# Attention radial weights from a plain input, y0 multiplied in PSUM by ScalarE, and two y copies moved in VectorE's order

## The chip, the cores and the metric

The program runs on one core of one Trainium2 chip. The metric is device time in microseconds from the first to the last instruction of that core; less is better.

## What is computed

The reference is two layers of an equivariant graph network. The first is attention over 206,250 edges; the change lies there. For each edge a radial vector of 16 numbers (`rbf`) is multiplied by `W_rbf` to give 224 weights, and these scale the edge's message by way of `y0` and `y1`, the edge's spherical harmonics:

```
w1 = rbf @ W_rbf                       # ss 64 | sv 64 | vs 32 | vv0 32 | vv1 32
out_s = concat[w_ss * s * y0,  w_vv0 * (v . y1) / sqrt3]
out_v = concat[(w_sv * s) y1,  w_vs * v * y0,  w_vv1 * cross(v, y1) / sqrt2]
```

So `y0` belongs to two of the five parts, `ss` and `vs`, which are 96 of the 224 columns. The rest of the layer (logits, softmax, values, a second product with `y`, the sum over edges) and the second layer stay as they are.

## The kernel before

`attention_edges` works through 404 tiles of 512 edges (`SUPER = 404`), each as 4 blocks of 128 edges with the edges in partitions. Every engine has one loop, unrolled four times, and its order is written out by hand. A step `t = m + d` in the body of iteration `m` says that this engine does that piece of work for tile `m + d`; so one iteration mixes pieces of some six tiles. Engines are tied by counting semaphores alone. "An iteration" below is one pass of an engine through this body.

The names that matter, with the lines of the kernel before:

- **SyncE** loads `rin` (L452), the gather indices, `y_early` (L460) and `y_late` (L466), and stores `hout` (L471). **GpSimd** gathers 4 + 4 blocks of node rows for each tile (L484, L487), and may start on a tile once VectorE has summed the tile four before it (semaphore `summed`, L586).
- **Radial weights.** `rin` holds, for each tile, 64 rows of 512 columns: on the left `rbf` twice, on the right y0 and ones. VectorE multiplies left by right into `rbfy` (L537). TensorE multiplies `rbfy` by `wy` into `b_w`, banks 0 and 1 of PSUM (L697); it first waits for VectorE's last reader of `b_w`, L556 (`first_done`). VectorE reads `b_w` one iteration later (L547 to L556) to make `first`.
- **TensorE's order from the weights on:** weights (L697), transposes of the second block of `second` (`turn2(t,1)`, L639), `maps(t,1)` (L647 to L649), third transposes (`turn2(t,2)`, L639 on `nodes`), then in the next body the first transposes of `first` (L630), `values_of(t,0)` (L657 to L659), more transposes, `values_of(t,1)`, `maps(t,0)`, `turn2(t,0)` (L639 on `ae_second`), and the weights again. `values_of(t,0)` waits until ScalarE has copied the third transposes out (`kept2`).
- **ScalarE's order over the same stretch:** `keep2(t,1)` (L729, copies the second transposes out of PSUM), four activations that scale `gated` by y0 (L781), `keep2(t,2)` (L729), `keep_maps(t,1)` (L718 to L720), `keep1(t,0)` (L725).
- **The small copies on VectorE:** `ya` (L534), `yb` (L575) and `yc` (L580) bring y values into bank 7 of PSUM, where the products with y (L514, L566, L602) read them.

The buffer `spare`, which the profile names `nodes`, holds `gated`.

Of the kernel before, what the change touches and what calls it, by code (L numbers as in the profile page):

```python
# [21 lines left out]
ALU = mybir.AluOpType  # L22
# [5 lines left out]
P = 128  # L28
# [352 lines left out]
def attention_edges(nc, g):  # L381

    w, psum, banks, io = g["w"], g["psum"], g["banks"], g["io"]
    with ExitStack() as ctx:
        def sb(name, shape, dt=F32):
            return ctx.enter_context(nc.sbuf_tensor(f"ae_{name}", shape, dt))

        def sem(name):
# [7 lines left out]
        rin = [sb(f"rin{u}", [64, 512]) for u in range(4)]  # L396
        rbfy = [sb(f"rbfy{u}", [64, 256]) for u in range(2)]
# [20 lines left out]
        ya_done, yb_done, yc_done, summed, spread, outer_done, cross_done, dot_done, first_done = (sem(x) for x in (  # L418
            "ya_done", "yb_done", "yc_done", "summed", "spread", "outer_done", "cross_done", "dot_done", "first_done"))
# [6 lines left out]
        kept, mapped_kept, scaled, kept2, values_kept, yy_kept, logit_kept = (sem(x) for x in (  # L426
            "kept", "mapped_kept", "scaled", "kept2", "values_kept", "yy_kept", "logit_kept"))
# [17 lines left out]
        with nc.Block() as block:  # L445
            @block.sync
            def _(sp):
                def body(m):
                    t = m + 4
                    if t.inside(SUPER):  # L450
                        wait(sp, spread, t.n - 3)
                        sp.dma_start(rin[t.slot4][:, :], io["rin"][t.n]).then_inc(rin_in[t.slot4], 16)  # L452
# [40 lines left out]
            def _(dve):  # L493
# [10 lines left out]
                def body(m):  # L504
# [26 lines left out]
                    if t.inside(SUPER):  # L531
                        dve.wait_ge(early_in[t.slot4], 16 * (t.quarter + 1))
                        wait(dve, outer_done, t.n)
                        dve.tensor_copy(ya, y_early[t.slot4][:, :, 1:6]).then_inc(ya_done, 1)  # L534
                        dve.wait_ge(rin_in[t.slot4], 16 * (t.quarter + 1))
                        wait(dve, pe_weights, t.n - 1)
                        dve.tensor_tensor(rbfy[t.slot][:, :], rin[t.slot4][:, 0:256], rin[t.slot4][:, 256:512], ALU.mult)\  # L537
                            .then_inc(spread, 1)
                    t = m
                    if t.inside(SUPER):  # L540
# [4 lines left out]
                        dve.wait_ge(pe_weights, t.n + 1)  # L545
                        wait(dve, pe_turned, 3 * t.n - 3)
                        dve.tensor_tensor(out[:, :, 0:384 - P].rearrange("p k (a c) -> p k a c", c=CS)[:, :, 0:4:3, :],  # L547
                                          b_w[:, :, 0:P].rearrange("p k (a c) -> p k a c", a=2),
                                          msg[:, :, 0:CS].unsqueeze(2).to_broadcast([P, 4, 2, CS]), ALU.mult)
                        dve.tensor_tensor(comps(out[:, :, 256:352]), b_w[:, :, 192:224].unsqueeze(2).to_broadcast(three),  # L550
                                          comps(msg[:, :, CS:C]), ALU.mult)
                        dve.wait_ge(cross_done, t.n + 1)
                        dve.tensor_tensor(comps(out[:, :, 96:192]), b_w[:, :, 160:192].unsqueeze(2).to_broadcast(three),
                                          cross[:, :, :, :], ALU.mult)
                        dve.wait_ge(dot_done, t.n + 1)
                        dve.tensor_tensor(out[:, :, CS:96], b_w[:, :, P:160], dot[:, :, :], ALU.mult).then_inc(first_done, 1)  # L556
# [31 lines left out]
                    if t.inside(SUPER):  # L588
# [7 lines left out]
                        dve.tensor_reduce(dot[:, :, :], diag[:, :, :, :].rearrange("p k x c -> p k c x"), AX, ALU.add).then_inc(rest_done, 1)  # L596
                    t = m + -4
# [28 lines left out]
            def _(pe):  # L626
# [35 lines left out]
                def body(m):  # L662
# [50 lines left out]
            def _(act):  # L713
# [24 lines left out]
                def body(m):  # L738
# [34 lines left out]
                    if t.inside(SUPER):  # L773
                        keep2(t, 1)
                    t = m + -2
# [14 lines left out]
                loop(act, body, 0, SUPER + 4, SUPER, 4)  # L790
# [498 lines left out]
def lay_pack(i):  # L1289
# [13 lines left out]
    for lo in (0, 32):  # L1303
        W["wy"][lo:lo + 16, 0:64], W["wy"][lo:lo + 16, 192:224] = ss, vs
        W["wy"][lo + 16:lo + 32, 64:128], W["wy"][lo + 16:lo + 32, 128:160], W["wy"][lo + 16:lo + 32, 160:192] = sv, vv0, vv1
# [40 lines left out]
def lay_inputs(i):  # L1346
# [16 lines left out]
    rbf = np.pad(np.asarray(i["edge_attr_16"]), ((0, E - EDGES), (0, 0))).reshape(SUPER, 2, 256, 16).transpose(0, 1, 3, 2)  # L1363
    y0 = np.broadcast_to(y[:, :, 0].reshape(SUPER, 2, 1, 256), rbf.shape)
    left = np.concatenate([rbf, rbf], 2).reshape(SUPER, 64, 256)
    right = np.concatenate([y0, np.ones_like(rbf)], 2).reshape(SUPER, 64, 256)
# [4 lines left out]
        rin=np.concatenate([left, right], 2), yall=y.reshape(4 * SUPER, P, 4).transpose(1, 0, 2),  # L1371
# [21 lines left out]
```

## Time and profile before

| | |
|---|---|
| median of 3 runs | 8659.92 us (8658.96 to 8663.35) |
| the profiled execution, own time | 8654.65 us |
| its span | 8652.9 us |
| granted clock of TensorE, mean | 0.943 |
| busy: TensorE / VectorE / ScalarE / GpSimd | 83% / 88% / 60% / 64% |
| the attention edge loop | about 264 to 4637 us of the span |

The span holds stages with different limits, so shares over the whole say little about the attention loop; the rows further down take that loop alone. Durations of neighbouring instructions on one engine overlap a little: where the time that an instruction costs its engine is wanted, read the distance from its start to the next start.

### The profile page before, as it was taken

The page shows a single profiled execution, that of the slowest core. Times are in us where ns is not written, and L with a number is a line of the kernel's source. Part 1 is how long each engine was busy: PE and PEld are TensorE (multiplying, and loading weights), DVE is VectorE, ACT ScalarE, POOL GpSimd, SP SyncE. Part 2 cuts the span into 40 slices and gives each one's busy share as a digit, 9 for nine tenths or more (in the row PEclk, how much of TensorE's full clock was granted, in tenths as well). Part 3 has the DMA queues.
Part 4 walks back from the last instruction along what each step waited for, and adds up shares of the span by engine and source line. Part 5 has one row for each costly group of instructions (what it writes and reads, how often), then busy time and mean ns, then how long its engine had stood idle before and what let it go on. Part 6 is the DMA issues. An engine that isn't in the chain of part 4 may idle for free. (4 is left out here: it accounts for less than half of the span.)

```text
span 8652.9 us, 204396 instructions
## 1 busy us (share of the span) xinstructions
PE 7203.1 (83%) x48374; PEld 5958.3 (69%) x48374; DVE 7624.6 (88%) x18883; ACT 5158.5 (60%) x17363; POOL 5527.0 (64%) x5949
## 2 busy tenths in 40 slices
PE   4799999999999999999996677756888888888885
PEld 2688888888888888888885566633555555555555
DVE  3799999999999999999998555534999999999993
ACT  1466666666666666666664211112777777777771
POOL 0677777777777777777772677702777777777750
PEclk5799999999999999999998999955999999999995
DMA  1343333333333333333331566601333333333330
GB/s 71 92 109 106 105 105 106 105 105 106 106 105 106 105 105 106 105 105 105 106 105 57 170 181 181 181 3 47 92 88 89 89 89 89 88 89 89 88 72 19
DMA packets 854921, 859.39 MB, mean 99 GB/s; under 512 B 480448, under 2 KB 637760, under 8 KB 854208
## 3 DMA queue, kind: packets, MB, share of 16 engines
q0 software_dynamic: 241920, 413.20, 19.6%
q1 hardware_dynamic: 612928, 445.36, 18.0%
q8 instruction: 28, 0.46, 0.0%
q14 instruction: 45, 0.37, 0.0%
HBM read 709.51 MB, written 148.44 MB: 99 GB/s over the span
## 5 line engine op out<-in xcount | busy, mean ns | idle before, releaser
L1157 POOL DMA_INDIRECT ce_node<-tab_conv,ce_idx x1808 | 1708.7, 945 | 1059.8 <-issue 654.3
L484 POOL DMA_INDIRECT ae_gsrc<-tab_src,ae_idx x1616 | 1537.2, 951 | 890.6 <-issue 449.7
L487 POOL DMA_INDIRECT ae_gdst<-tab_dst,ae_idx x1616 | 1635.6, 1012 | 541.3 <-issue 539.4
L1247 PE MATMUL psum<-ce_prod,ce_plain 128*128 128x384 f32 x3616 | 1540.5, 508 | 337.8 <-DVE ce_prod L1220 275.1
L1232 ACT ACTIVATE ce_prod<-ce_raw,ce_y 128x64 f32<-128x64 f32 x5424 | 1465.1, 333 | 0.0
L1230 ACT ACTIVATE ce_prod<-ce_raw,ce_y 128x160 f32<-128x160 f32 x1808 | 753.4, 417 | 527.9 <-DVE ce_raw L1179 527.9
L729 ACT ACTIVATE ae_second_t<-psum 128x512 f32<-128x512 f32 x1212 | 731.5, 604 | 502.2 <-PE psum L639 496.2
L1249 PEld LDWEIGHTS psum<-ce_prod,ce_plain 128*128 128x128 f32 x3616 | 688.0, 190 | 479.9 <-issue 2.1
L1247 PEld LDWEIGHTS psum<-ce_prod,ce_plain 128*128 128x128 f32 x3616 | 547.2, 191 | 484.8 <-DVE ce_plain L1208 346.1
L647 PE MATMUL psum<-pack_sb,ae_first_t 128*128 128x200 f32 x3232 | 851.8, 345 | 2.2 <-ACT ae_first_t L725 2.0
L1008 PE MATMUL psum<-ag_exval,ag_hot 128*128 128x164 f32 x3616 | 615.3, 314 | 223.9 <-issue 116.2
L657 PE MATMUL psum<-pack_sb,ae_second_t 128*128 128x96 f32 x3232 | 664.4, 287 | 129.0 <-ACT ae_second_t L729 125.0
L1008 PEld LDWEIGHTS psum<-ag_exval,ag_hot 128*128 128x128 f32 x3616 | 514.6, 190 | 324.6 <-DVE agg L997 131.3
L725 ACT ACTIVATE ae_first_t<-psum 128x512 f32<-128x512 f32 (+1 forms) x1212 | 690.2, 607 | 40.8 <-PE psum L630 40.5
L697 PE MATMUL psum<-pack_sb,ae_rbfy 32*128 32x224 f32 x3232 | 418.2, 372 | 297.7 <-DVE ae_first L556 276.2
L630 PE MATMUL psum<-pack_sb,ae_first 128*128 128x128 f32 (+1 forms) x4848 | 664.7, 274 | 0.0
L657 PEld LDWEIGHTS psum<-pack_sb,ae_second_t 128*128 128x128 f32 x3232 | 486.0, 190 | 240.9 <-issue 164.6
L1249 PE MATMUL psum<-ce_prod,ce_plain 128*128 128x96 f32 x3616 | 647.0, 261 | 0.0
L649 PE MATMUL psum<-pack_sb,ae_first_t 96*128 96x96 f32 x3232 | 626.8, 276 | 0.0
L659 PE MATMUL psum<-pack_sb,ae_second_t 128*128 128x96 f32 x3232 | 625.4, 275 | 0.0
L658 PE MATMUL psum<-pack_sb,ae_second_t 128*128 128x96 f32 x3232 | 625.3, 275 | 0.0
L735 ACT ACTIVATE ae_values<-psum 128x256 f32<-128x256 f32 x808 | 310.5, 384 | 522.1 <-PE psum L659 522.1
(179 smaller groups left out, 19883.6 us busy)
## 6 DMA issues: line engine op xcount, KB each, us to landing
ag_val<-h_dram SPq DMA_DIRECT2D x452, 320.0 KB, 3.2
h_dram<-ae_hout SPq DMA_DIRECT2D x404, 320.0 KB, 2.2
ce_query<-in_query SPq DMA_DIRECT2D x452, 128.0 KB
ae_rin<-in_rin SPq DMA_DIRECT2D x404, 128.0 KB
ce_node<-tab_conv,ce_idx POOLq DMA_INDIRECT x1808
ae_gsrc<-tab_src,ae_idx POOLq DMA_INDIRECT x1616
ae_gdst<-tab_dst,ae_idx POOLq DMA_INDIRECT x1616
nodes<-in_x SPq DMA_DIRECT2D x2, 3920.0 KB, 14.0
```

What stands on the lines that cost most here:

```text
L484: pool.indirect_dma_start(gsrc[t.slot4][:, k, :], None, g["tab_src"], bass.IndirectOffsetOnAxis(ap=idx[t.slot4][:, k:k + 1], axis=0))\
L487: pool.indirect_dma_start(gdst[t.slot4][:, k, :], None, g["tab_dst"], bass.IndirectOffsetOnAxis(ap=idx[t.slot4][:, 4 + k:5 + k], axis=0))\
L647: pe.matmul(b_m[:, i, 0:200], first_t[0][:, e], w("m1_0"), start=True, stop=False)
L657: pe.matmul(b_h[:, i, 0:96], second_t[0][:, e], w("m2_0"), start=True, stop=False, skip_group_check=True)
L725: act.activation(first_t[b][0:rows, :], b_t[b % 2][0:rows, :], ACT.Copy).then_inc(kept, 1)
L729: act.activation(second_t[b][:, :], b_t[(b + 1) % 2][:, :], ACT.Copy).then_inc(kept2, 1)
L1008: ins = pe.matmul(banks[t.slot4][:, 0:W], hot[t.slot4][:, k, :], exval[t.slot4][:, k, :], start=(k == 0), stop=(k == 3))
L1157: pool.indirect_dma_start(node[t.slot8][:, k, :], None, g["tab_conv"], bass.IndirectOffsetOnAxis(ap=idx[t.slot8][:, k:k + 1], axis=0))\
L1230: act.activation(prod[t.slot][:, k, 0:160], raw[t.slot][:, k, 0:160], ACT.Identity, scale=y[t.slot8][:, k, 0:1])
L1232: ins = act.activation(prod[t.slot][:, k, 192 + 96 * x:256 + 96 * x], raw[t.slot][:, k, 160:WW], ACT.Identity, scale=y[t.slot8][:, k, x + ...
L1247: pe.matmul(b_a[t.slot], plain[t.slot4][:, k, :], prod[t.slot][:, k, 96:480], start=(k == 0), stop=False, skip_group_check=True)
L1249: ins = pe.matmul(b_a[t.slot][:, 96:384].rearrange("p (x c) -> p x c", x=3)[:, :, CS:96], plain[t.slot4][:, k, :], prod[t.slot][:, k, 0:96 ...
```

## The change

`rin` becomes 64 rows of 256 columns: `rbf` and 16 rows of zeros for each half, with no y0 in it. VectorE's multiplication (L537) and its buffer go, and TensorE takes `rin` straight from the load. The columns of the weights are put in another order, `vs, ss, sv, vv0, vv1`, so that the 96 that need y0 stand first. ScalarE then multiplies these 96 columns by y0, in place in PSUM, with four activations for a tile, and signals `weighted`, for which VectorE waits in the place of `pe_weights`. On VectorE the copy `yb` moves from between L569 and L586 to behind the reduction L596; the copy `yc` moves from behind `yb` to behind `ya`, where L537 stood. ScalarE's loop starts one body earlier.

```diff
-        rin = [sb(f"rin{u}", [64, 512]) for u in range(4)]
-        rbfy = [sb(f"rbfy{u}", [64, 256]) for u in range(2)]
+        rin = [sb(f"rin{u}", [64, 256]) for u in range(4)]
...
@@ SyncE
-                        wait(sp, spread, t.n - 3)
+                        wait(sp, pe_weights, t.n - 3)
                         sp.dma_start(rin[t.slot4][:, :], io["rin"][t.n]).then_inc(rin_in[t.slot4], 16)
@@ VectorE
                         dve.tensor_copy(ya, y_early[t.slot4][:, :, 1:6]).then_inc(ya_done, 1)
-                        dve.wait_ge(rin_in[t.slot4], 16 * (t.quarter + 1))
-                        wait(dve, pe_weights, t.n - 1)
-                        dve.tensor_tensor(rbfy[t.slot][:, :], rin[t.slot4][:, 0:256], rin[t.slot4][:, 256:512], ALU.mult)\
-                            .then_inc(spread, 1)
+                    t = m + -4
+                    if t.inside(SUPER):
+                        dve.wait_ge(late_in[t.slot4], 16 * (t.quarter + 1))
+                        wait(dve, path2_done, t.n)
+                        dve.tensor_copy(yc, y_late[t.slot4][:, :, 2:5]).then_inc(yc_done, 1)
...
-                        dve.wait_ge(pe_weights, t.n + 1)
+                        dve.wait_ge(weighted, t.n + 1)
...
-                    t = m + -1
-                    if t.inside(SUPER):
-                        dve.wait_ge(early_in[t.slot4], 16 * (t.quarter + 1))
-                        wait(dve, outer2_done, t.n)
-                        dve.tensor_copy(yb, y_early[t.slot4][:, :, 1:6]).then_inc(yb_done, 1)
-                    t = m + -4
-                    if t.inside(SUPER):
-                        dve.wait_ge(late_in[t.slot4], 16 * (t.quarter + 1))
-                        wait(dve, path2_done, t.n)
-                        dve.tensor_copy(yc, y_late[t.slot4][:, :, 2:5]).then_inc(yc_done, 1)
...
                         dve.tensor_reduce(dot[:, :, :], diag[:, :, :, :].rearrange("p k x c -> p k c x"), AX, ALU.add).then_inc(rest_done, 1)
+                    t = m + -1
+                    if t.inside(SUPER):
+                        dve.wait_ge(early_in[t.slot4], 16 * (t.quarter + 1))
+                        wait(dve, outer2_done, t.n)
+                        dve.tensor_copy(yb, y_early[t.slot4][:, :, 1:6]).then_inc(yb_done, 1)
@@ TensorE
-                        pe.wait_ge(spread, t.n + 1)
+                        pe.wait_ge(rin_in[t.slot4], 16 * (t.quarter + 1))
...
-                            ins = pe.matmul(b_w[:, k, :], rbfy[t.slot][q:q + 32, e:e + P], w("wy")[q:q + 32, :], start=True, stop=True)
+                            ins = pe.matmul(b_w[:, k, :], rin[t.slot4][q:q + 32, e:e + P], w("wy")[q:q + 32, :], start=True, stop=True)
@@ ScalarE, between keep2(m - 3, 1) and the scaling of gated for m - 2
+                    t = m + 1
+                    if t.inside(SUPER):
+                        act.wait_ge(pe_weights, t.n + 1)
+                        act.wait_ge(early_in[t.slot4], 16 * (t.quarter + 1))
+                        for k in range(4):
+                            ins = act.activation(b_w[:, k, 0:96], b_w[:, k, 0:96], ACT.Identity, scale=y_early[t.slot4][:, k, 0:1])
+                        ins.then_inc(weighted, 1)
...
-                loop(act, body, 0, SUPER + 4, SUPER, 4)
+                loop(act, body, -1, SUPER + 4, SUPER, 4)
```

ScalarE's order of before, in the looped body, from the copies of logit and yy to the copies of the maps; `ae_second_t` is the copied transposes, `nodes` read by L781 is `gated`:

```order
L766 ACTIVATE alpha<-ae_logit 128x16 [waits ae_logit_done]
L771 ACTIVATE ae_yy<-yy 128x4 [waits ae_outer2_done]
L729 ACTIVATE ae_second_t<-psum 128x512 [waits ae_pe_turned2]
L781 ACTIVATE ae_second<-nodes,ae_y_late 128x192 [waits ae_pe_turned2,ae_late_in2,ae_gate_done]
L781 ACTIVATE ae_second<-nodes,ae_y_late 128x192 x3
L729 ACTIVATE ae_second_t<-psum 128x512 [waits ae_pe_turned2]
L718 ACTIVATE ae_mapped<-psum 128x2x72 [waits ae_pe_mapped]
```

The same place in ScalarE's order of the change (line numbers shift by five, L724 is `keep2`, L783 the scaling of `gated`):

```order
L761 ACTIVATE alpha<-ae_logit 128x16 [waits ae_logit_done]
L766 ACTIVATE ae_yy<-yy 128x4 [waits ae_outer2_done]
L724 ACTIVATE ae_second_t<-psum 128x512 [waits ae_pe_turned2]
L775 ACTIVATE psum<-psum,ae_y_early 128x96 [waits ae_early_in1,ae_pe_weights]
L775 ACTIVATE psum<-psum,ae_y_early 128x96 x3
L783 ACTIVATE ae_second<-nodes,ae_y_late 128x192 [waits ae_pe_turned2,ae_late_in2,ae_gate_done]
L783 ACTIVATE ae_second<-nodes,ae_y_late 128x192 x3
L724 ACTIVATE ae_second_t<-psum 128x512 [waits ae_pe_turned2]
L713 ACTIVATE ae_mapped<-psum 128x2x72 [waits ae_pe_mapped]
```

Four activations now stand between the copy of the second transposes and the scaling of `gated`, ahead of the copy of the third transposes.

VectorE's order of before, from the end of the second set of products with y to the third:

```order
L569 TENSOR_TENSOR ae_bent<-nodes,ae_yy 128x128 [waits ae_bent_done,ae_yy_kept]
L575 COPY psum<-ae_y_early 128x20 [waits ae_outer2_done,ae_early_in0]
L580 COPY psum<-ae_y_late 128x12 [waits ae_path2_done,ae_late_in1]
L586 TENSOR_TENSOR ae_msg<-ae_gsrc,ae_gdst 128x640 [waits ae_outer_done,ae_first_done,ae_gathered2]
L593 TENSOR_TENSOR nodes<-ae_plus,psum 128x4x2x32 [waits ae_first_done,ae_pe_turned2,ae_outer2_done]
L595 TENSOR_TENSOR ae_second<-ae_plus,psum 128x4x32
L596 TENSOR_REDUCE ae_dot<-ae_diag 128x128
L602 TENSOR_TENSOR ae_path<-ae_values,psum 128x384 [waits ae_values_done,ae_yc_done,ae_values_kept]
```

The same place in VectorE's order of the change:

```order
L569 TENSOR_TENSOR ae_bent<-nodes,ae_yy 128x128 [waits ae_bent_done,ae_yy_kept]
L576 TENSOR_TENSOR ae_msg<-ae_gsrc,ae_gdst 128x640 [waits ae_outer_done,ae_first_done,ae_gathered2]
L583 TENSOR_TENSOR nodes<-ae_plus,psum 128x4x2x32 [waits ae_first_done,ae_pe_turned2,ae_outer2_done]
L585 TENSOR_TENSOR ae_second<-ae_plus,psum 128x4x32
L586 TENSOR_REDUCE ae_dot<-ae_diag 128x128
L591 COPY psum<-ae_y_early 128x20 [waits ae_outer2_done,ae_early_in0]
L597 TENSOR_TENSOR ae_path<-ae_values,psum 128x384 [waits ae_values_done,ae_yc_done,ae_values_kept]
```

Both copies have gone from between the product L569 and the sum of the gathered rows; one of them now stands ahead of the third product.

## Rows read from the trace of the kernel before

**Rows 1.** Windows: PE, PEld, DVE, ACT, POOL busy; clock, DMA share, GB/s.

```profile
320.00:4410.00 4090.00, 3723.18 (x30180) 3433.20 (x30177) 4043.47 (x10561) 2747.59 (x8300) 2977.02 (x3033) 1.00 0.40 106
```

**Rows 2.** One line's instructions over the whole span: the sum L586, once a tile.

```profile
L586 DVE TENSOR_TENSOR ae_msg<-ae_gsrc,ae_gdst x404: 809/826/827, 263.9 to 4637.1; 128x640 f32<-128x640 f32 x135
```

**Rows 3.** Waits from 1000 to 4000 us: total, times, longest.

```profile
ACT ae_second_t L729 <- PE psum L639: 345.1, 277, 1.4
...
PE psum L697 <- DVE ae_first L556: 183.9, 277, 0.8
...
PE psum L657 <- ACT ae_second_t L729: 85.9, 277, 0.3
```

**Rows 4.** Timeline of one iteration, TensorE (PE, PEld) and ScalarE.

```profile
2010.72 0.68 PEld L697 LDWEIGHTS psum<-pack_sb,ae_rbfy 32*128 32x128 f32 x8 [0.84 <-DVE ae_first L556]
...
2012.37 0.60 ACT L729 ACTIVATE ae_second_t<-psum 128x512 f32<-128x512 f32 x1 [1.18 <-PE psum L639]
...
2012.87 1.48 ACT L781 ACTIVATE ae_second<-nodes,ae_y_late 128x192 f32<-128x192 f32 x4
...
2013.61 0.47 PEld L639 LDWEIGHTS psum<-pack_sb,nodes 128*128 128x128 f32 x4
2013.72 0.60 PE L639 MATMUL psum<-pack_sb,nodes 128*128 128x128 f32 x4
...
2014.06 0.47 PEld L630 LDWEIGHTS psum<-pack_sb,ae_first 128*128 128x128 f32 x4
...
2014.36 0.60 ACT L729 ACTIVATE ae_second_t<-psum 128x512 f32<-128x512 f32 x1
...
2015.09 0.30 PEld L657 LDWEIGHTS psum<-pack_sb,ae_second_t 128*128 128x128 f32 x2 [0.56 <-issue]
...
2020.19 0.47 PEld L639 LDWEIGHTS psum<-pack_sb,ae_second 128*128 128x128 f32 x4
```

**Rows 5.** Timeline of VectorE around L537 and around the two copies.

```profile
2007.96 0.17 DVE L534 COPY psum<-ae_y_early 128x20 f32<-128x20 f32 x1
2008.04 0.40 DVE L537 TENSOR_TENSOR ae_rbfy<-ae_rin 64x256 f32<-64x256 f32 x1
2008.37 0.57 DVE L543 TENSOR_REDUCE ae_dot<-ae_diag 128x128 f32<-128x384 f32 x1
...
2011.99 0.27 DVE L569 TENSOR_TENSOR ae_bent<-nodes,ae_yy 128x128 f32<-128x128 f32 x1
2012.36 0.18 DVE L575 COPY psum<-ae_y_early 128x20 f32<-128x20 f32 x1
2012.49 0.17 DVE L580 COPY psum<-ae_y_late 128x12 f32<-128x12 f32 x1
2012.70 0.83 DVE L586 TENSOR_TENSOR ae_msg<-ae_gsrc,ae_gdst 128x640 f32<-128x640 f32 x1
```

**Rows 6.** Timeline of GpSimd: the first and the last gather of one tile.

```profile
2003.44 0.94 POOL L484 DMA_INDIRECT ae_gsrc<-tab_src,ae_idx  x1 [0.84 <-DVE ae_msg L586]
...
2012.55 0.95 POOL L487 DMA_INDIRECT ae_gdst<-tab_dst,ae_idx  x1 [0.30 <-issue]
```

**Rows 7.** Timeline of ScalarE elsewhere: L299, L301 and L1232 scale by a column.

```profile
84.72 0.35 ACT L301 ACTIVATE tab_feat<-psum,pack_sb 96x128 f32<-96x128 f32 x1
84.97 0.45 ACT L299 ACTIVATE tab_feat<-psum,pack_sb 64x128 f32<-64x128 f32 x1
...
6012.57 0.81 ACT L1232 ACTIVATE ce_prod<-ce_raw,ce_y 128x64 f32<-128x64 f32 x3
```

**Rows 8.** Timeline of ScalarE: a plain copy out of PSUM, and its successor.

```profile
2014.86 0.28 ACT L718 ACTIVATE ae_mapped<-psum 128x144 f32<-128x144 f32 x1
2015.03 0.34 ACT L719 ACTIVATE nodes<-psum 128x192 f32<-128x192 f32 x1
```

**Rows 9.** Groups by line on ScalarE, whole span: count, busy us, mean ns, idle.

```profile
L1232 ACT ACTIVATE ce_prod<-ce_raw,ce_y 128x64 f32<-128x64 f32 x5424 | 1465.1, 333 | 0.0
...
L781 ACT ACTIVATE ae_second<-nodes,ae_y_late 128x192 f32<-128x192 f32 x1616 | 598.0, 444 | 0.0
```

More of the change, by code:

```diff
@@ L416, in attention_edges @@
         filled, may_gather = sem("filled"), sem("may_gather")
-        ya_done, yb_done, yc_done, summed, spread, outer_done, cross_done, dot_done, first_done = (sem(x) for x in (
-            "ya_done", "yb_done", "yc_done", "summed", "spread", "outer_done", "cross_done", "dot_done", "first_done"))
+        ya_done, yb_done, yc_done, summed, outer_done, cross_done, dot_done, first_done = (sem(x) for x in (
+            "ya_done", "yb_done", "yc_done", "summed", "outer_done", "cross_done", "dot_done", "first_done"))
         gate_done, outer2_done, bent_done, rest_done, scored_done, logit_done, path2_done, values_done = (sem(x) for x in (
@@ L424, in attention_edges @@
             "pe_weights", "pe_turned", "pe_mapped", "pe_turned2", "pe_values"))
-        kept, mapped_kept, scaled, kept2, values_kept, yy_kept, logit_kept = (sem(x) for x in (
-            "kept", "mapped_kept", "scaled", "kept2", "values_kept", "yy_kept", "logit_kept"))
+        weighted, kept, mapped_kept, scaled, kept2, values_kept, yy_kept, logit_kept = (sem(x) for x in (
+            "weighted", "kept", "mapped_kept", "scaled", "kept2", "values_kept", "yy_kept", "logit_kept"))
         b_w = psum[:, 0:2, :].rearrange("p b (k c) -> p (b k) c", c=256)[:, :, 0:WY]
@@ L544, in body @@
                             .then_inc(dot_done, 1)
-                        dve.wait_ge(pe_weights, t.n + 1)
+                        dve.wait_ge(weighted, t.n + 1)
                         wait(dve, pe_turned, 3 * t.n - 3)
                         dve.tensor_tensor(out[:, :, 0:384 - P].rearrange("p k (a c) -> p k a c", c=CS)[:, :, 0:4:3, :],
-                                          b_w[:, :, 0:P].rearrange("p k (a c) -> p k a c", a=2),
+                                          b_w[:, :, 32:160].rearrange("p k (a c) -> p k a c", a=2),
                                           msg[:, :, 0:CS].unsqueeze(2).to_broadcast([P, 4, 2, CS]), ALU.mult)
-                        dve.tensor_tensor(comps(out[:, :, 256:352]), b_w[:, :, 192:224].unsqueeze(2).to_broadcast(three),
+                        dve.tensor_tensor(comps(out[:, :, 256:352]), b_w[:, :, 0:32].unsqueeze(2).to_broadcast(three),
                                           comps(msg[:, :, CS:C]), ALU.mult)
                         dve.wait_ge(cross_done, t.n + 1)
-                        dve.tensor_tensor(comps(out[:, :, 96:192]), b_w[:, :, 160:192].unsqueeze(2).to_broadcast(three),
+                        dve.tensor_tensor(comps(out[:, :, 96:192]), b_w[:, :, 192:224].unsqueeze(2).to_broadcast(three),
                                           cross[:, :, :, :], ALU.mult)
                         dve.wait_ge(dot_done, t.n + 1)
-                        dve.tensor_tensor(out[:, :, CS:96], b_w[:, :, P:160], dot[:, :, :], ALU.mult).then_inc(first_done, 1)
+                        dve.tensor_tensor(out[:, :, CS:96], b_w[:, :, 160:192], dot[:, :, :], ALU.mult).then_inc(first_done, 1)
                     t = m + -2
@@ L1361, in lay_inputs @@
     ey6 = y.reshape(SUPER, 4, P, 4)[..., [0, 1, 2, 3, 1, 2]].transpose(0, 2, 1, 3).reshape(SUPER, P, 24)
[L1363 to L1366, printed above, removed]
+    rbf = np.pad(np.asarray(i["edge_attr_16"]), ((0, E - EDGES), (0, 16))).reshape(SUPER, 2, 256, 32).transpose(0, 1, 3, 2)
     query = np.pad(np.asarray(i["edge_attr_64"]), ((0, E - EDGES), (0, 0))).reshape(SUPER, 2, 256, 64)
@@ L1370, in lay_inputs @@
         pack=lay_pack(i), x=x, eidx=eidx, ey6=ey6, sdst=sdst, dst3=dst3,
-        rin=np.concatenate([left, right], 2), yall=y.reshape(4 * SUPER, P, 4).transpose(1, 0, 2),
+        rin=rbf.reshape(SUPER, 64, 256), yall=y.reshape(4 * SUPER, P, 4).transpose(1, 0, 2),
         query=query)
```

3 lines of the change are left out of this document (1 added, 2 removed).

## The prediction

> **What bounds the kernel now.** I read the page first, for where the engines are busy: VectorE has the most, TensorE is close behind (the table above). Over the whole span that mixes stages, so next I took the attention loop alone. There VectorE is busy 4043 of 4090 us (98.9%), TensorE 3723 (91.0%), GpSimd 2977 (72.8%), ScalarE 2748 (67.2%), with TensorE's granted clock at 1.00 throughout [rows 1]. The length of an iteration comes from one line that runs once a tile: 404 sums, first at 263.9 and last at 4637.1 us, so (4637.1 - 263.9) / 403 = 10.85 us [rows 2]. Then the list of waits: VectorE has none in it. TensorE waits for VectorE's L556 in every iteration, 183.9 / 277 = 0.66 us, and for ScalarE's copy of the transposes, 85.9 / 277 = 0.31 us; ScalarE waits 1.25 us for TensorE [rows 3]; GpSimd waits for VectorE's sum [rows 6]. Three engines wait for VectorE or for each other and VectorE for none: VectorE sets the pace, with TensorE only some tenths behind it. So whatever VectorE sheds is gained only until the next loop of dependences is as long. There are three to measure.
>
> **VectorE's own length afterwards.** L537 costs it the distance to the next start, 2008.37 - 2008.04 = 0.33 us. From L569 to L586 it takes 12.70 - 11.99 = 0.71 us, though the product, 0.27 us long, is followed only by two copies on 20 and 12 columns: L575 starts 0.10 us after L569 has ended, because it waits for that end [rows 5]. With both copies gone the sum waits only for older things; I put it 0.25 us behind L569, which gives 0.46. The copies come back elsewhere at 0.08 (L534 to L537) to 0.21 us each (L580 to L586) [rows 5]; I take 0.25 for both. The net is -0.33 - 0.46 + 0.25 = -0.54, that is 10.31 us; with the ends 10.2 to 10.45.
>
> **GpSimd's own length.** Its eight gathers start 9.11 us apart from first to last (2003.44 to 2012.55), seven steps, or 1.30 each; the eighth step brings 10.4 us. It now waits 0.84 us at the head of each tile instead of the usual 0.30, for the sum that VectorE moves earlier [rows 6]. It would be at most 10.4 us, and it is three tiles ahead.
>
> **The ring of TensorE and ScalarE.** This is the one the change lengthens. Weights (L697) load at 2010.72. Behind them on TensorE stand the second transposes; ScalarE starts to copy these at 2012.37, so 1.65 us after. Its next start is 0.50 later (2012.87). Four scalings of `gated` take 1.48 with the last at full length, 0.444 [rows 9], so one step is (1.48 - 0.444) / 3 = 0.345. Then comes the copy of the third transposes, 0.60 long, and 0.13 us after its end (2014.96) TensorE loads for `values_of` at 2015.09. From there it runs without a wait to 2020.19, and four more transposes at the pace of 2013.61 to 2014.06 bring it to the next weights: 5.10 + 0.45 = 5.55 us [rows 4]. The third copy starts at 2014.36 today because the third transposes end only at 13.72 + 0.60 = 14.32 [rows 4]; with ScalarE later that end is no longer what it waits for, and the four scalings count 4 x 0.345 = 1.38. All together 1.65 + 0.50 + 1.38 + 0.60 + 0.13 + 5.55 = 9.81 us, plus w for the four new activations, which are queued just ahead of the scalings. Today this ring has about 1 us to spare against 10.85; everything hangs on w.
>
> **The price of w.** The trace has no scaling within PSUM. Nearest is L301, which reads PSUM, scales by a column of SBUF and has 128 columns: its successor starts 84.97 - 84.72 = 0.25 us later [rows 7]. Fewer columns are cheaper: L1232 at 64 columns steps by (0.81 - 0.333) / 2 = 0.24, L781 at 192 by 0.345, so (0.345 - 0.24) / 128 = 0.00082 us a column [rows 4, 7, 9]. For 96 columns that is 0.25 - 32 x 0.00082 = 0.22, and w = 4 x 0.22 = 0.89. From below, a plain copy out of PSUM steps by 15.03 - 14.86 = 0.17 at 144 columns [rows 8], 0.13 at 96, so w = 0.52. From above, priced as a scaling that reads SBUF, 0.24 + 32 x 0.00082 = 0.27 and w = 1.07. The value taken is that of L301: same source, same kind of scale, only the destination differs. The wait for `pe_weights` ahead of them costs nothing, since TensorE has done the second transposes, which stand behind the weights, before ScalarE even begins its copy; `y_early` was loaded two iterations before. Behind the four are queued the scalings of `gated`, the third copy and both `keep` copies; TensorE's `values_of` waits for the third copy.
>
> The Trainium skill, "ScalarE: Activation LUTs", section "What ACT_TABLE_LOAD costs", gives an activation 186 ns + 0.833 ns a column, 93 ns more for a scale column, and 93 ns of overlap with the next. By that 96 columns cost 0.27 us each, an estimate of w = 1.06. L301's 0.35 us is under the 0.386 that this rule gives for 128 columns. The sum by the rule is the second rival's.
>
> **The rest at nothing.** `rin` has half the bytes and is waited for by TensorE instead of VectorE; it is loaded four tiles ahead. SyncE's waits move: `rin` now follows `pe_weights`, about 3 us later in its round than L537 was, `y_early` follows the later `yb`; each is needed two or more iterations on, so 10 us or more of cover against a few. Should the cover of `rin` go, TensorE would stand at the weights for the lateness of the load. VectorE's new wait for `weighted`: the four are done about 1.65 + 0.50 + 0.89 = 3.0 us after the weights began, and VectorE's readers of `b_w` come behind L543, which starts at 2008.37 [rows 5], or 2019.2 one iteration later, 8.5 us after that mark. TensorE's weights take the same time, since neither rows nor columns of the matmul change.
>
> **The sum.** The ring is 9.81 + 0.89 = 10.70 us, longer than VectorE's 10.31 and GpSimd's 10.4, so it becomes the pace. 10.85 - 10.70 = 0.15 us, times 404 is 61 us. Against the profiled execution's own 8654.65 that is 8594; the median of the runs shown is 5 us above it, so **8599 us**, 0.7% less. VectorE sheds 218 us, and some 157 of them turn into its new waits. The measurement of this kernel can tell about 0.2%, 17 us, from no change, so the sign turns at 10.81 for faster and at 10.89 for slower, that is w = 1.00 and 1.08.
>
> **Rivals.**
>
> 1. *The ring does not close.* If the activations cost as little as a plain copy, w = 0.52, the ring is 10.33 us and GpSimd's 10.4 sets the pace: 0.45 x 404 = 182 us, 8478. Against it speaks L301, which steps by 0.25 us at 128 columns where the plain copy steps by 0.17 at 144 [rows 7, 8]: scaling by a column is not free. Chance 0.09.
> 2. *The activations cost as those that read SBUF.* Then w = 1.07, the ring 10.88, +0.03 x 404 = +12 us: 8672, within 0.2%, and the kernel has only changed its bound. This is what the page of the Trainium skill named above comes to. Chance 0.15.
> 3. *Slower: the four in-place activations don't overlap.* All four read and write the same two banks; if each had to end before the next reads, each costs its duration, about 0.35 - 0.03 = 0.32 us by L301 [rows 7], w = 1.29, the ring 11.10, +0.25 x 404 = +101 us: 8761. Slower is decided from w = 1.08 on, 0.27 an activation. For it: nothing in the trace reads and writes PSUM on ScalarE. Against: plain copies that follow one another through one pair of banks overlap freely [rows 8]. Chance 0.11.
>
> **Chances and range.** The forecast has 0.65: w from 0.80 to 1.00, so 10.61 to 10.81 us, 8563 to 8644. Faster by over 0.2% takes the forecast and rival 1, less what of the forecast lies at its upper edge: 0.72. Within 0.2% 0.16, slower 0.12. The range goes from part of the way to rival 1 up over rival 2, 8520 to 8682, and leaves out rival 3 and most of rival 1.
>
> **What would show it.** Distance of L576, the sum, from tile to tile: 10.70. The new line L775: 1616 instructions, mean about 320 ns, step 0.22. In the list of waits TensorE's wait for VectorE's L556 is gone; its wait for ScalarE's L724 grows from 0.31 to some 0.8 us an iteration, since TensorE's own work is 10.85 - 0.66 - 0.31 = 9.88. VectorE's busy share in the loop falls from 98.9% to about 96%, with a wait for ScalarE's maps or for `weighted`. ScalarE's third copy starts right behind L783, with no wait for TensorE. L569 to the sum: 0.25 instead of 0.71. If VectorE is still without waits and the iteration is under 10.5, the ring was mis-sized; if the step of L775 is over 0.27, rival 3 holds. The forecast is wrong too if TensorE's stretch from `values_of` to the weights, 5.55 here, meets new waits of its own once VectorE is earlier.

## The result and the profile after

The changed kernel takes 8676.86 us (median of 16 runs, 8674.66 to 8681.44), the kernel before in the same measurement 8660.35 us (16 runs). The ratio is 1.002, with a 95% interval of 1.0012 to 1.0027. The forecast was 8599 us, 0.7% less; what came is 0.2% more. It is inside the range of 8520 to 8682, but the interval puts it on the other side of no change.

The iteration first. The sum of the gathered rows, now L576, once a tile, over the whole span of the changed kernel:

```profile
L576 DVE TENSOR_TENSOR ae_msg<-ae_gsrc,ae_gdst x404: 807/817/827, 262.7 to 4655.8; 128x640 f32<-128x640 f32 x135
```

(4655.8 - 262.7) / 403 = 10.90 us, where it was 10.85 [rows 2]. From first to last sum the loop is 19.9 us longer; the medians differ by 16.5 us and the two profiled spans by 26.3. The windows of the same stretch as [rows 1], with the same columns:

```profile
320.00:4410.00 4090.00, 3676.82 (x30011) 3406.49 (x30010) 3870.52 (x10132) 3030.45 (x9758) 3024.84 (x3019) 1.00 0.37 99
```

VectorE has fallen from 98.9% to 94.6% (about 96% was forecast) and ScalarE has risen from 67.2% to 74.1%; TensorE's granted clock is 1.00 in both. So VectorE did shed its work, and it was no longer busy all the time. Who waits for whom, from 1000 to 4000 us of the changed kernel (total, times, longest):

```profile
PE psum L652 <- ACT ae_second_t L724: 302.6, 275, 1.1
...
DVE nodes L520 <- ACT ae_mapped L715: 161.5, 275, 0.8
ACT ae_second_t L724 <- PE psum L634: 141.8, 275, 0.5
```

TensorE's wait for VectorE's L556 [rows 3] is gone from the list. Its wait for ScalarE's third copy has grown from 0.31 to 302.6 / 275 = 1.10 us an iteration (some 0.8 was forecast), and VectorE, which waited for nobody, now waits 0.59 us for ScalarE's copies of the maps. These rows fit the forecast's picture, that the pace has passed from VectorE to the ring of TensorE and ScalarE; the experiments below test it. The ring is longer than forecast. It can be read off one iteration of the changed kernel, start by start (columns: start, length, engine, line):

```profile
2006.12 0.47 PEld L634 LDWEIGHTS psum<-pack_sb,ae_second 128*128 128x128 f32 x4
2006.76 0.68 PEld L692 LDWEIGHTS psum<-pack_sb,ae_rin 32*128 32x128 f32 x8 [0.17 <-issue]
...
2007.71 0.42 PEld L634 LDWEIGHTS psum<-pack_sb,ae_second 128*128 128x128 f32 x4 [0.28 <-issue]
...
2008.41 0.60 ACT L724 ACTIVATE ae_second_t<-psum 128x512 f32<-128x512 f32 x1 [0.52 <-PE psum L634]
2008.90 1.00 ACT L775 ACTIVATE psum<-psum,ae_y_early 128x96 f32<-128x96 f32 x4
2009.80 1.51 ACT L783 ACTIVATE ae_second<-nodes,ae_y_late 128x192 f32<-128x192 f32 x4
2011.18 0.61 ACT L724 ACTIVATE ae_second_t<-psum 128x512 f32<-128x512 f32 x1
...
2011.91 0.30 PEld L652 LDWEIGHTS psum<-pack_sb,ae_second_t 128*128 128x128 f32 x2 [1.35 <-issue]
...
2017.02 0.48 PEld L634 LDWEIGHTS psum<-pack_sb,ae_second 128*128 128x128 f32 x4
2017.66 0.68 PEld L692 LDWEIGHTS psum<-pack_sb,ae_rin 32*128 32x128 f32 x8 [0.16 <-issue]
```

| step of the ring | forecast | measured |
|---|---|---|
| weights to ScalarE's second copy | 1.65 | 1.65 |
| that copy | 0.50 | 0.49 |
| four activations in PSUM (w) | 0.89 | 0.90 |
| four scalings of `gated` | 1.38 | 1.38 |
| third copy, and TensorE's load after it | 0.73 | 0.73 |
| TensorE from `values_of` to `turn2(t,0)` | 5.10 | 5.11 |
| from `turn2(t,0)` to the weights | 0.45 | 0.64 |
| sum | 10.70 | 10.90 |

Six of seven steps came within 0.01 us. The seventh is 0.19 us too short. The row to look at is L692: it begins 0.64 us after the four transposes' first load, and 0.16 us after the end of their last, with no engine named as releaser. In the kernel before, TensorE stood there anyway, 0.84 us for VectorE [rows 4], and the 0.19 us lay under that wait.

VectorE came out close to the forecast. From L569 to the sum it now takes 0.20 us (0.25 was forecast), and the copies, L591 and L538, cost 0.08 us each in their new places (0.25 for both was forecast):

```profile
2006.50 0.28 DVE L569 TENSOR_TENSOR ae_bent<-nodes,ae_yy 128x128 f32<-128x128 f32 x1
2006.70 0.82 DVE L576 TENSOR_TENSOR ae_msg<-ae_gsrc,ae_gdst 128x640 f32<-128x640 f32 x1
...
2008.47 0.17 DVE L591 COPY psum<-ae_y_early 128x20 f32<-128x20 f32 x1
2008.55 0.54 DVE L597 TENSOR_TENSOR ae_path<-ae_values,psum 128x384 f32<-128x384 f32 x1
...
2010.87 0.55 DVE L513 TENSOR_TENSOR ae_plus<-ae_msg,psum 128x384 f32<-128x384 f32 x1
2011.33 0.56 DVE L513 TENSOR_TENSOR psum<-ae_msg,psum 128x384 f32<-128x384 f32 x1
2012.65 0.69 DVE L520 TENSOR_TENSOR nodes<-ae_mapped,nodes 128x512 f32<-128x512 f32 x1 [0.76 <-ACT ae_mapped L715]
...
2013.87 0.16 DVE L538 COPY psum<-ae_y_late 128x12 f32<-128x12 f32 x1
2013.95 0.58 DVE L543 TENSOR_REDUCE ae_dot<-ae_diag 128x128 f32<-128x384 f32 x1
```

L520 starts 1.32 us after the last L513 instead of the 0.46 at which these follow one another; in this iteration VectorE loses 0.86 us there. The mean step over the loop, taken from all such starts, is 1.14 us, so 0.68 us lost, and VectorE's own work is 10.90 - 0.68 = 10.22 us an iteration (10.31 forecast).

### The profile page after: what moved, and what is told of

The parts are those of the page before. It is cut to its first block and busy times, and to the rows that moved or that the text cites. A ratio compares the mean times of both kernels' runs of the same rounds, so it can differ in the third digit from the quotient of the medians.

```text
span 8679.2 us, 205804 instructions
## 1 busy us (share of the span) xinstructions
PE 7175.0 (83%) x48374; PEld 5950.2 (69%) x48374; DVE 7461.0 (86%) x18479; ACT 5479.1 (63%) x18979; POOL 5591.7 (64%) x5949
## 5 line engine op out<-in xcount | busy, mean ns | idle before, releaser
L486 POOL DMA_INDIRECT ae_gdst<-tab_dst,ae_idx x1616 | 1701.8, 1053 | 530.5 <-issue 530.5
L1249 PE MATMUL psum<-ce_prod,ce_plain 128*128 128x384 f32 x3616 | 1539.8, 508 | 338.1 <-DVE ce_prod L1222 275.4
L1232 ACT ACTIVATE ce_prod<-ce_raw,ce_y 128x160 f32<-128x160 f32 x1808 | 753.2, 417 | 526.9 <-DVE ce_raw L1181 526.9
L1249 PEld LDWEIGHTS psum<-ce_prod,ce_plain 128*128 128x128 f32 x3616 | 547.0, 191 | 485.1 <-DVE ce_plain L1210 343.1
L724 ACT ACTIVATE ae_second_t<-psum 128x512 f32<-128x512 f32 x1212 | 737.9, 609 | 208.5 <-PE psum L634 208.4
L720 ACT ACTIVATE ae_first_t<-psum 128x512 f32<-128x512 f32 (+1 forms) x1212 | 699.8, 617 | 1.1 <-PE psum L625 1.1
L783 ACT ACTIVATE ae_second<-nodes,ae_y_late 128x192 f32<-128x192 f32 x1616 | 608.2, 474 | 0.0
```

The lines of the kernel that those rows point to most:

```text
L486: pool.indirect_dma_start(gdst[t.slot4][:, k, :], None, g["tab_dst"], bass.IndirectOffsetOnAxis(ap=idx[t.slot4][:, 4 + k:5 + k], axis=0))\
L720: act.activation(first_t[b][0:rows, :], b_t[b % 2][0:rows, :], ACT.Copy).then_inc(kept, 1)
L724: act.activation(second_t[b][:, :], b_t[(b + 1) % 2][:, :], ACT.Copy).then_inc(kept2, 1)
L1232: act.activation(prod[t.slot][:, k, 0:160], raw[t.slot][:, k, 0:160], ACT.Identity, scale=y[t.slot8][:, k, 0:1])
L1249: pe.matmul(b_a[t.slot], plain[t.slot4][:, k, :], prod[t.slot][:, k, 96:480], start=(k == 0), stop=False, skip_group_check=True)
```

## The experiments

Two theories stand at the start. **The ring**: the loop of TensorE and ScalarE in the table above is the pace, each activation stands in it with its full step, and 0.19 us of it is the way into the radial weights. **VectorE by way of the maps**: the pace is VectorE's chain, which now waits at L520 for ScalarE's copies of the maps, and these stand behind the four activations. Both fit a time of 8677 us.

Of 18 runs, three give times that can be set beside the change's: e5, e6 and e16. The other 15 ran on chips where the kernel before itself took 12,200 to 13,000 us instead of 8660. There an iteration takes 17.8 to 19.9 us on average, in every kernel, and ScalarE idles for microseconds ahead of copies for which the trace names no engine of the core as releaser. Two of its rows in e17:

```profile
3884.53 0.60 ACT L725 ACTIVATE ae_first_t<-psum 128x512 f32<-128x512 f32 x1 [2.27 <-remote]
3887.39 0.59 ACT L725 ACTIVATE ae_first_t<-psum 96x512 f32<-96x512 f32 x1 [2.26 <-remote]
```

TensorE idles too, and its granted clock goes to and fro between 1.00 and 0.50, its levels of 2.4 and 1.2 GHz. Windows of e17, with the columns of [rows 1]:

```profile
320.00:4410.00 4090.00, 2884.18 (x18057) 2615.88 (x18057) 2409.85 (x6342) 1675.93 (x4971) 1795.27 (x1812) 0.76 0.23 63
...
3876.00:3882.00 6.00, 0.00 (x0) 0.00 (x0) 2.21 (x7) 0.29 (x2) 4.48 (x6) 0.50 0.28 64
```

Over the attention loop the clock is 0.76 of full speed where it was 1.00, and in the 6 us ahead of the rows above TensorE runs no matmul and stands at 0.50. These delays drown the ring, so a ratio of two such times says nothing about this question. From those runs I use distances between neighbouring instructions, at a granted clock of 1.00, and whole iterations without a stall. Two of these stand at the end of every run: the last two distances from sum to sum, at a granted clock of 1.00 and, in these 15, with all gathers done. Where the whole loop is undisturbed they agree with its mean: 10.91 us in the changed kernel, 10.35 in e5 and 10.45 in e16. Only in the kernel before do they not, with 11.16 and 10.80.

**The activations behind the third copy** (e3, and e5 where it counts). The block is taken out from ahead of the scalings and put behind `keep2(t, 2)`:

```diff
 keep2(m - 3, 1)
-four activations on b_w (t = m + 1), weighted + 1
 scaling of gated (t = m - 2)
 keep2(m - 3, 2)
+four activations on b_w (t = m + 1), weighted + 1
 keep_maps(m - 1, 1)
```

> The changed kernel with the four in-place activations moved behind the copy of the third transposes (and ahead of the copies of the maps), so that TensorE no longer waits for them. Theory of the ring: it shrinks by 0.89 to 10.0 us, plus about 0.2 because the copy of the first transposes is now late for TensorE; then VectorE's 10.3 or GpSimd's 10.4 us is the pace: about 8677 - 0.5 x 404 = 8475 us. Rival (the pace is the wait of VectorE for ScalarE's copies of the maps, which stand behind the activations in either order): unchanged, 10.90 us and 8677 us.

> The kernel of e3 once more, since on the chip of the first four runs the kernel before itself took 12828 us. The changed kernel with the four in-place activations behind the copy of the third transposes. Theory of the ring: about 10.4 us an iteration, 8475 us. Rival (the pace is VectorE's wait for ScalarE's copies of the maps, which stand behind the activations in either order): unchanged, 10.90 us and 8677 us.

e3 is one of the 15 (12545 us); its last two iterations take 10.35 us. e5 took 8458.34 us against 8655.42 before on the same chip, ratio 0.9773 (0.9757 to 0.979). The sum's line and two waits of e5:

```profile
L576 DVE TENSOR_TENSOR ae_msg<-ae_gsrc,ae_gdst x404: 807/820/843, 263.2 to 4436.0; 128x640 f32<-128x640 f32 x135
```

```profile
PE psum L652 <- ACT ae_second_t L724: 89.9, 290, 0.3
...
PEld psum L625 <- ACT ae_first_t L720: 74.7, 290, 0.3
...
DVE nodes L520 <- ACT ae_mapped L715: 15.0, 73, 0.2
```

10.35 us an iteration. The activations still stand ahead of the maps here, so the second theory falls: it had forecast no change. TensorE's wait for the third copy is back to 0.31 us, and the wait on L720 (74.7 / 290 = 0.26 us) is the lateness of the first transposes' copy that the expectation names. So the ring can be read off this kernel too:

```profile
2003.90 0.68 PEld L692 LDWEIGHTS psum<-pack_sb,ae_rin 32*128 32x128 f32 x8 [0.17 <-issue]
...
2006.90 0.60 PE L634 MATMUL psum<-pack_sb,nodes 128*128 128x128 f32 x4
...
2007.54 0.60 ACT L724 ACTIVATE ae_second_t<-psum 128x512 f32<-128x512 f32 x1
...
2008.26 0.30 PEld L652 LDWEIGHTS psum<-pack_sb,ae_second_t 128*128 128x128 f32 x2 [0.56 <-issue]
...
2014.25 0.68 PEld L692 LDWEIGHTS psum<-pack_sb,ae_rin 32*128 32x128 f32 x8 [0.16 <-issue]
```

From the weights to the third copy it takes 3.64 us, 0.12 more than 1.65 + 0.49 + 1.38 = 3.52, because the third transposes end only at 2007.50, as in the kernel before; 0.72 to TensorE's load; and 5.99 to the next weights, 0.24 more than 5.11 + 0.64 = 5.75, because of L720. Together that is 10.35. The four activations have not left the ring altogether: of their 0.90 us they still cost 0.24, by way of L720. GpSimd waits for VectorE no more, and its gathers fill the iteration; but it is not what holds the pace, since e3 keeps to 10.35 us in its last two iterations, with all gathers done. This version is the fastest of the study, 2.3% under the kernel before.

**Half the activations** (e9, e11, e13, and e16 where it counts):

```diff
-                        for k in range(4):
+                        for k in range(2):
                             ins = act.activation(b_w[:, k, 0:96], b_w[:, k, 0:96], ACT.Identity, scale=y_early[t.slot4][:, k, 0:1])
```

> The changed kernel with two of the four in-place activations left out (blocks 2 and 3 of each tile keep weights without y0, so the output differs). Theory of the ring: each activation stands in the ring with its full step of 0.223 us, so 10.90 - 0.45 = 10.45 us an iteration, 8677 - 180 = 8497 us, and VectorE's wait for the maps shrinks by the same. Rival (something else of the change holds the pace and ScalarE's time is only partly in it): less than half of that, over 8590 us.

Of the three repeats, e11, e13 and e16:

> The kernel of e9 once more: the changed kernel with two of the four in-place activations left out (blocks 2 and 3 keep weights without y0). Theory of the ring: 10.90 - 0.45 = 10.45 us an iteration, 8677 - 180 = 8497 us. Rival (something else of the change holds the pace): over 8590 us.

> The kernel of e9 once more: the changed kernel with two of the four in-place activations left out (blocks 2 and 3 keep weights without y0). Theory of the ring: 10.90 - 0.45 = 10.45 us an iteration, 8677 - 180 = 8497 us. Rival (something else of the change holds the pace): over 8590 us.

> The kernel of e9 once more: the changed kernel with two of the four in-place activations left out (blocks 2 and 3 keep weights without y0). Theory of the ring: 10.90 - 0.45 = 10.45 us an iteration, 8677 - 180 = 8497 us. Rival (something else of the change holds the pace): over 8590 us.

e9, e11 and e13 are among the 15 (12527, 12518 and 12267 us); their last two iterations take 10.44 to 10.45 us. e16 took 8493.9 us against 8656.79, ratio 0.9811 (0.9795 to 0.9828); 8497 was expected. The sum's line of e16, and TensorE's wait for the third copy:

```profile
L576 DVE TENSOR_TENSOR ae_msg<-ae_gsrc,ae_gdst x404: 805/819/826, 262.3 to 4472.4; 128x640 f32<-128x640 f32 x135
```

```profile
PE psum L652 <- ACT ae_second_t L724: 184.0, 288, 0.7
```

10.45 us: two activations fewer take 0.454 us off an iteration, 0.227 each, against a step of 0.223 to 0.225. TensorE's wait has fallen by as much, from 1.10 to 184.0 / 288 = 0.64 us. Each activation stands in the pace in full. That alone would also fit the theory of the maps, behind fewer activations; with e5, which rules that theory out, it leaves the ring as the cause, with the size of w. GpSimd does not hold e16 either: e13 has the same 10.45 us with all gathers done.

**TensorE's waits moved ahead of the transposes** (e4, and e6 where it counts). The 0.19 us could be the two waits that stand directly ahead of the radial weights:

```diff
+                        pe.wait_ge(rin_in[t.slot4], 16 * (t.quarter + 1))      # for t = m + 1
+                        wait(pe, first_done, t.n)
                         turn2(m - 3, 0)
-                        pe.wait_ge(rin_in[t.slot4], 16 * (t.quarter + 1))
-                        wait(pe, first_done, t.n)
                         radial weights (t = m + 1)
```

> The changed kernel with TensorE's two waits for the radial weights (the load of rin, VectorE's first_done) taken four transposes earlier, so that no wait stands directly ahead of the weights. In the changed kernel the first weight load comes 0.307 us after the last transpose's load, where 0.11 is the pace: 0.20 us of the ring. If the waits are what costs, the gap falls to about 0.11 and the iteration to 10.70 us, 8597 us. If it is the step from full-height to 32-row operands, the gap stays 0.30 and the time 8677 us.

> The kernel of e4 once more, for the same reason. TensorE's two waits for the radial weights four transposes earlier. If the waits cost the 0.20 us ahead of the weights, the gap from the last transpose's load to the first weight load falls from 0.307 to about 0.11 and the iteration to 10.70 us, 8597 us. If it is the step from full-height to 32-row operands, gap 0.30 and 8677 us.

e4 is one of the 15 (12505 us; last two iterations 10.92 and 10.93 us). e6 took 8679.4 us against 8655.42, ratio 1.0028 (1.0018 to 1.0038). TensorE's weight loads in e6:

```profile
2009.23 0.47 PEld L634 LDWEIGHTS psum<-pack_sb,ae_second 128*128 128x128 f32 x4
2009.87 0.68 PEld L694 LDWEIGHTS psum<-pack_sb,ae_rin 32*128 32x128 f32 x8 [0.17 <-issue]
```

Still 0.64 us, where 0.44 would have come if the waits were the cause. The waits are not it.

**Radial weights at full height** (e10). `rin` gets 128 rows a block, 16 of them filled, and the four matmuls no longer use 32-row pieces of TensorE:

```diff
-                        for k in (0, 2, 1, 3):
-                            q, e = 32 * (k // 2), P * (k % 2)
-                            ins = pe.matmul(b_w[:, k, :], rin[t.slot4][q:q + 32, e:e + P], w("wy")[q:q + 32, :], start=True, stop=True)
+                        for k in range(4):
+                            ins = pe.matmul(b_w[:, k, :], rin[t.slot4][:, P * k:P * k + P], w("wy"), start=True, stop=True)
```

> The changed kernel with the radial matmuls on all 128 rows of TensorE: each block of 128 edges has its 16 rows of rbf and 112 rows of zeros, so the four matmuls no longer run in pairs on 32-row groups, and rin is 256 KB a tile. If the 0.20 us ahead of the weights is the step from full height to 32-row operands, the gap from the last transpose's load to the first weight load falls from 0.307 to about 0.11, and the 0.28 us behind the weights goes as well; the matmuls themselves take about 8 x 0.19 = 1.5 us where they took 0.95, so the iteration is 10.90 - 0.20 + 0.57 = 11.27 us, 8827 us. If it is the buffer or the line and not the height, the gap stays at 0.30 and the iteration is 11.5 us.

Its time is one of those not used (12330 us, the kernel before 12781). Its weight loads, in a stretch without a stall at a granted clock of 1.00:

```profile
3008.25 0.48 PEld L634 LDWEIGHTS psum<-pack_sb,ae_second 128*128 128x128 f32 x4
3008.69 1.44 PEld L691 LDWEIGHTS psum<-pack_sb,ae_rin 128*128 128x128 f32 x8
3010.13 0.55 PEld L634 LDWEIGHTS psum<-pack_sb,ae_second 128*128 128x128 f32 x4
```

From the transposes to the weights it is 0.44 us, the pace of four transposes, and the idle time on both sides of the weights has gone. Over the 400 places in each trace where transposes of `second` are followed by the radial weights, the median distance from the last load to the first is 0.108 us here and 0.307 us in the changed kernel, in e5 and in e6. So the 0.20 us belong to the step from full-height to 32-row operands, not to a wait, a buffer or a line. The weights themselves take 1.44 us here, from load to next load, where they take 0.95 there (2006.76 to 2007.71). The last two iterations take 11.32 and 11.33 us, near the 11.27 expected from the height and not the 11.5 expected from the buffer or the line; so this is no version to keep.

**The copies alone** (e1, e7, e12, e14, e17): the kernel before with `yb` behind L596 and `yc` behind `ya`.

> The kernel before with the two copies yb and yc at their new places and nothing else; the rbfy product on VectorE stays. Theory of the ring (TensorE and ScalarE pass each other weights, transposes, scalings and values; without the four new activations that ring is 10.90 - 0.89 = 10.01 us): VectorE stays the pace and gets shorter by 0.46 - 0.25 = 0.21 us, so 10.64 us an iteration, 8660 - 85 = 8575 us. Rival, that the moved copies are what made the change slow (a copy is late for its reader): slower than 8660.

> The kernel of e1 once more. The kernel before with the copies yb and yc at their new places and nothing else. Theory of the ring (without the four activations it is 10.90 - 0.89 = 10.01 us): VectorE stays the pace and gets shorter by 0.21 us, so 10.64 us an iteration, 8575 us. Rival, that a moved copy is late for its reader: slower than 8660.

> The kernel of e1 once more: the kernel before with the copies yb and yc at their new places and nothing else. Theory of the ring: VectorE stays the pace and gets shorter by 0.21 us, 10.64 us an iteration, 8575 us. Rival, that a moved copy is late for its reader: slower than 8660.

> The kernel of e1 once more: the kernel before with the copies yb and yc at their new places and nothing else. Theory of the ring: VectorE stays the pace and gets shorter by 0.21 us, 10.64 us an iteration, 8575 us. Rival, that a moved copy is late for its reader: slower than 8660.

> The kernel of e1 once more: the kernel before with the copies yb and yc at their new places and nothing else. Theory of the ring: VectorE stays the pace; by the stretches without a stall in the runs of this kernel so far it is 10.53 us an iteration, 8660 - 0.31 x 404 = 8533 us. Rival, that a moved copy is late for its reader: slower than 8660.

All five runs are among the 15, so there is no time to use: 13035, 12999, 13105, 12356 and 12402 us, with the kernel before at 12828, 12781, 12785, 12399 and 12403; the first three are 1 to 3% slower than the kernel before, the last two within 0.6% of it. What can be read is an iteration without a stall, from two sums of e17:

```profile
3865.75 0.82 DVE L581 TENSOR_TENSOR ae_msg<-ae_gsrc,ae_gdst 128x640 f32<-128x640 f32 x1
...
3876.28 0.82 DVE L581 TENSOR_TENSOR ae_msg<-ae_gsrc,ae_gdst 128x640 f32<-128x640 f32 x1
```

10.53 us; about a quarter of all iterations in e17 have this length, and the last two of all five runs take 10.52 to 10.54. In them VectorE does its whole round without waiting, so its own work with the copies moved is 10.53 us, 0.32 less than 10.85 and more than the 0.21 expected at first (e17 was already expected at 10.53, from the runs before it). A moved copy that came late for its reader would show in it. Why three of the five come out slower on those chips is not shown. That the kernel would gain 0.32 x 404 = 129 us by the copies alone follows only if nothing else is longer than 10.53; the ring without activations, 10.90 - 0.90 = 10.00, is not, but the time itself stays unmeasured.

**The weights alone** (e2, e8, e15, e18): the changed kernel with the copies back in their old places.

> The changed kernel with yb and yc back at their old places. Theory of the ring: VectorE has about 0.6 us of waiting in each iteration, the copies cost it 0.21 more, the ring does not contain them: 10.90 us an iteration as in the changed kernel, 8677 us. Rival (VectorE's own order still sets the pace, by way of its wait for ScalarE's maps): 10.90 + 0.21 = 11.1 us, 8760 us.

> The kernel of e2 once more. The changed kernel with yb and yc back at their old places. Theory of the ring: the copies lie on VectorE, which has 0.6 us of waiting an iteration, so 10.90 us as in the changed kernel, 8677 us. Rival (VectorE's own order still sets the pace by way of its wait for ScalarE's maps): 11.1 us, 8760 us.

> The kernel of e2 once more: the changed kernel with yb and yc back at their old places. Theory of the ring: the ring does not contain them, so 10.90 us an iteration as in the changed kernel, 8677 us. Rival (VectorE's own order still sets the pace by way of its wait for ScalarE's maps): 11.1 us, 8760 us.

> The kernel of e2 once more: the changed kernel with yb and yc back at their old places. Theory of the ring: the ring does not contain them, so 10.90 us an iteration as in the changed kernel, 8677 us. Rival (VectorE's own order still sets the pace by way of its wait for ScalarE's maps): 10.90 + 0.31 = 11.2 us, 8800 us.

There is no time to use: the four runs are among the 15 (12588, 12576, 12320 and 12331 us), and unlike in e17 hardly an iteration is without a stall. But the last two are. From e18:

```profile
7496.92 0.82 DVE L581 TENSOR_TENSOR ae_msg<-ae_gsrc,ae_gdst 128x640 f32<-128x640 f32 x1
...
7502.36 0.69 DVE L520 TENSOR_TENSOR nodes<-ae_mapped,nodes 128x512 f32<-128x512 f32 x1 [0.33 <-ACT ae_mapped L715]
...
7507.82 0.82 DVE L581 TENSOR_TENSOR ae_msg<-ae_gsrc,ae_gdst 128x640 f32<-128x640 f32 x1
...
7518.73 0.83 DVE L581 TENSOR_TENSOR ae_msg<-ae_gsrc,ae_gdst 128x640 f32<-128x640 f32 x1
```

10.90 and 10.91 us, and 10.90 to 10.92 in all four runs: the 10.90 of the ring, not the 11.1 to 11.2 of its rival. The copies' old places cost VectorE 0.3 us more, and its wait at L520 is shorter by as much, 0.33 us where the last iterations of the changed kernel have 0.61. So inside the changed kernel the two moved copies bring nothing. They would count beside a shorter ring, as in e5: 10.22 + 0.3 = 10.5 us of VectorE is more than its 10.35. No run shows that.

## Why the prediction was wrong

*What bounds the kernel now*: right. VectorE, with TensorE close behind; moving its two copies alone took 0.3 us off an iteration.

*VectorE's own length afterwards*, 10.31: it is 10.22. Over the loop the way from L569 to the sum took 0.66 us on average, less than the 0.71 of [rows 5], and takes 0.20 now: a fall of 0.45, as good as the 0.46 forecast from a long start and a late end. The two copies cost 0.15 together instead of 0.25. 10.85 - 0.33 - 0.45 + 0.15 = 10.22.

*GpSimd's own length*, at most 10.4: in e5 it has an iteration of 10.35 us and waits for nobody, so this held.

*The ring takes over*: right, and shown by e5 and e16, against the theory that ran through VectorE and the maps.

*The price of w*, 0.89 with ends 0.52 and 1.07: it is 0.90, and four times the step of 0.223 to 0.225. Taking the one row with the same source and the same kind of scale (L301 [rows 7]) was right. The 0.27 us an activation by the Trainium skill, "ScalarE: Activation LUTs", section "What ACT_TABLE_LOAD costs", an estimate for 96 columns, was too much here. The Trainium skill, "Perfetto Trace Analysis", section "Optimizing Scalar/DVE Operations", gives ScalarE some 93 ns for each instruction on SBUF and some 51 ns on PSUM; the 0.04 us between 0.27 and 0.225 agree with that.

*The ring's length without w*, 9.81: **this is the step that failed**. It was 10.00. The sentence "four more transposes at the pace of 2013.61 to 2014.06 bring it to the next weights" carried the pace of transposes into an instruction of another shape. In the kernel before, that place could not show its price, since TensorE was waiting there for VectorE anyway. The prediction did name this stretch among its signs of being wrong, but only for new waits, and put nothing on it. Two places of the trace of before held the price of such a step. Behind the same weights TensorE's loads stood idle for 0.28 us, which lies inside the 1.65 of the first step of the ring:

```profile
2011.68 0.42 PEld L639 LDWEIGHTS psum<-pack_sb,ae_second 128*128 128x128 f32 x4 [0.28 <-issue]
```

And in the second layer TensorE goes the same way from full-height to 64-row operands, at a place where the trace shows no wait. TensorE's weight loads of the kernel before:

```profile
7005.81 0.51 PEld L1249 LDWEIGHTS psum<-ce_prod,ce_plain 128*128 128x128 f32 x2
7006.24 0.30 PEld L1247 LDWEIGHTS psum<-ce_prod,ce_plain 128*128 128x128 f32 x2
7006.67 0.51 PEld L1249 LDWEIGHTS psum<-ce_prod,ce_plain 128*128 128x128 f32 x2
7007.28 0.68 PEld L1259 LDWEIGHTS psum<-pack_sb,ce_query 64*128 64x128 f32 x8
```

A pair of L1249 is followed by L1247 after 0.43 us and by the 64-row L1259 after 0.61, and the median of 450 such places is 0.61 too: 0.18 us for the step. With it the sum would have been 9.81 + 0.18 + 0.89 = 10.88 us, +12 us, and no change the forecast.

*The rivals*: the second, 8672 us, gave nearly the time that came, by a mechanism that did not: it had w = 1.07. The first and the third are out by the same measurement of w. That the range held the time is luck in part: its upper end was set by rival 2, not by any doubt about the rest of the ring.

*The size*: an error of 0.19 us in a ring of 10.9, under 2%, turned a gain of 0.15 us into a loss of 0.05. The chance of 0.72 for faster rested on w alone and left the rest of the ring without an uncertainty of its own.

## What to carry to other kernels

When an edit takes work off the engine that sets the pace and puts it on another, write down the loop of dependences through that other engine, start to start, before counting any gain. The same four activations cost 0.90 us an iteration ahead of the copy that TensorE waits for and 0.24 behind it (8677 against 8458 us). An engine's wait hides whatever its next instruction would cost at the start: when the wait is going to vanish, look for the same pair of instructions at a place in the trace where nothing is waited for.

## What the runs showed of the hardware

TensorE pays about 0.20 us to go from full-height to 32-row operands (0.307 us from load to load instead of 0.108), and 0.18 us to 64-row operands. The 0.28 us of idle loads behind the 32-row weights are gone too at full height. Moving the waits (e6) changed neither.

ScalarE, reading and writing the same columns of PSUM with a scale column from SBUF, steps by 0.223 us at 96 columns with a mean length of 321 ns, so each of the four starts some 0.1 us before the one ahead of it has ended. What follows them costs its step unchanged (0.345 us for L783), though its mean length in the trace is 474 ns instead of 444.

On several chips the same program took some 12,200 to 13,000 us. There ScalarE idles for microseconds ahead of copies, for which the trace names only a remote releaser, TensorE has stretches without a matmul, and its granted clock alternates between 1.00 and 0.50 (0.76 over the attention loop of e17, 1.00 in the kernels at 8660 us). What holds ScalarE there stays open.
